# Projection stage of an attention and FFN kernel: a ring of four x tiles in place of two, loads issued four batches ahead

## What is computed

```python
def attn(x):                      # on layernorm(x)
    q, k, v = proj(Wq, bq), proj(Wk, bk), proj(Wv, bv)          # B, H, S, 8
    idx = clip(pos[None, :] - pos[:, None], -20, 20) + 20
    attn1 = einsum('bhqd,bhkd->bhqk', q, k)
    attn2 = einsum('bhqd,qkd->bhqk', q, rel_k[idx])
    attn = softmax((attn1 + attn2) / sqrt(8))
    w1 = einsum('bhqk,bhkd->bhqd', attn, v)
    w2 = einsum('bhqk,qkd->bhqd', attn, rel_v[idx])
    return merge(w1 + w2) @ Wo.T + bo
x = x + attn(layernorm(x))
x = x + ffn(layernorm(x))         # silu(x Wg) * (x Wu), then Wd; weights int / 127
```

## Time and profile before

| | us |
|---|---|
| median of 3 runs | 1351.07 (1350.78 to 1351.37) |
| the profiled execution, its own time | 1343.95 |
| its span, first to last instruction | 1342.2 |
| projection stage, about | 0 to 140 |
| attention, about | 140 to 1180 |
| output, about | 1180 to 1342 |
| busy over the span: PE, DVE, ACT, POOL | 1238.7, 915.1, 755.4, 569.9 |

### The profile page before, as it was taken

How to read it: one execution, slowest core, us unless ns; L and a number is a source line. 1 busy time by engine, 2 the same in 40 slices (tenths; PEclk the granted TensorE clock), 3 DMA queues, 4 the chain that set the end, 5 groups by cost and what they waited for, 6 DMA issues and landing times. The chain is left out here.

```text
span 1342.2 us, 71473 instructions
## 1 busy us (share of the span) xinstructions
PE 1238.7 (92%) x32608; PEld 924.2 (69%) x32608; DVE 915.1 (68%) x1780; ACT 755.4 (56%) x1414; POOL 569.9 (42%) x1047
## 2 busy tenths in 40 slices
PE   4878599999999999999999999999999999999998
PEld 3555267777777777777777777777777777766766
DVE  5766876767777777676777767677777676246664
ACT  5867155656656556565665656566565565623332
POOL 5866345343444444343435343434444443212221
PEclk9989589999999999999999999999999999989999
DMA  4655310111011111102021111121111110022221
GB/s 136 197 186 195 90 31 19 49 30 57 28 48 42 34 46 32 53 24 56 20 56 33 50 38 48 38 56 39 45 42 34 48 28 12 11 57 81 80 86 48
DMA packets 101557, 77.24 MB, mean 58 GB/s; under 512 B 13256, under 2 KB 97032, under 8 KB 101256
## 3 DMA queue, kind: packets, MB, share of 16 engines
q1 hardware_dynamic: 101256, 72.67, 18.4%
HBM read 44.86 MB, written 26.21 MB: 53 GB/s over the span
## 5 line engine op out<-in xcount | busy, mean ns | idle before, releaser
L1117 DVE TENSOR_REDUCE b_mx<-b_a 128x1 f32<-128x512 f32 x1024 | 658.4, 685 | 221.7 <-PE b_a L831 217.5
L1062 ACT ACTIVATE b_p<-b_s 128x512 f32<-128x512 f32 x1024 | 569.9, 596 | 393.8 <-PE b_s L873 308.1
L923 PE MATMUL b_pv<-b_p,vg 128*16 128x128 f32 x8192 | 292.9, 275 | 1.1 <-issue 1.0
L791 POOL TENSOR_TENSOR qd<-q,one 48x512 bf16<-48x512 bf16 x256 | 266.2, 1040 | 27.7 <-POOLq L287 2.8
L873 PE MATMUL b_s<-qd,z 112*128 112x32 bf16 (+1 forms) x6016 | 250.5, 189 | 3.7 <-issue 3.3
L768 POOL TENSOR_TENSOR b_np<-b_db,one 128x16 bf16<-128x16 bf16 x192 | 39.1, 264 | 466.9 <-DVE b_mx L1117 463.9
L831 PE MATMUL b_a<-k,q 48*128 48x512 bf16 x1024 | 203.6, 393 | 31.5 <-DVE b_mx L1117 11.5
L873 PEld LDWEIGHTS b_s<-qd,z 112*128 112x128 bf16 (+1 forms) x6016 | 205.3, 98 | 15.1 <-issue 5.2
L923 PEld LDWEIGHTS b_pv<-b_p,vg 128*16 128x16 f32 x8192 | 200.5, 96 | 20.6 <-issue 2.9
L857 PE MATMUL b_s<-q,k 54*128 54x64 bf16 (+3 forms) x4608 | 188.2, 201 | 6.9 <-ACT b_p L1062 4.5
L857 PEld LDWEIGHTS b_s<-q,k 54*128 54x128 bf16 (+1 forms) x4608 | 126.7, 95 | 92.7 <-PE b_s L857 29.4
(11 more groups left out here) (142 smaller groups left out, 1270.8 us busy)
## 6 DMA issues: line engine op xcount, KB each, us to landing
x<-in_x SPq DMA_DIRECT2D x32, 256.0 KB, 3.3
scratch_qop<-a_parts SPq DMA_DIRECT2D x16, 384.0 KB, 2.5
scratch_kop<-a_parts SPq DMA_DIRECT2D x16, 384.0 KB, 3.2
k<-scratch_kop SPq DMA_DIRECT2D x32, 192.0 KB
q<-scratch_qop SPq DMA_DIRECT2D x32, 192.0 KB
scratch_v<-a_vr SPq DMA_DIRECT2D x16, 256.0 KB, 3.2
k<-scratch_kop SPq DMA_DIRECT2D x32, 128.0 KB
q<-scratch_qop SPq DMA_DIRECT2D x32, 128.0 KB
```

Source lines behind the costliest of these rows:

```text
L791: nc.gpsimd.tensor_tensor(dst, src, one, ALU.mult).then_inc(s["qd_ready"], 1)
L923: nc.tensor.matmul(PV[32 * a:32 * a + V16, g * P:(g + 1) * P], v[:, 0 if t <= i else 1, t, h, :], PR[at.c % 2][:, t, h, :], start=(t == 0 ...
L1062: nc.scalar.activation(out, src, ACT.Exp, scale=SCALE).then_inc(s["p_ready"], 1)
L1117: nc.vector.tensor_reduce(MX[v.c % 2][:, h:h + 1], PA[(n + hp) % NBANK][:, :], AX_X, ALU.max, negate=True).then_inc(s["a_used"], 1)
```

## The change

The projection takes x tiles from a ring of four: the two tiles x and the two tiles xa. Batch b uses tile b mod 4, each tile with a semaphore of its own. SP issues the loads of batches 2 and 3 at the start of the stage, before it waits for anything and before the constants; the load amid the constants goes away. In step n it waits for "xn" of batch n and loads batch n+4. The waits of DVE count the loads of the new semaphores. Nothing else is changed: same instructions, same sizes, same number of loads.

```diff
--- before.py
+++ after.py
@@ -25,6 +25,7 @@
 FC = F // P
 EPS = 1e-5
 NOUT = 2 + 2
+XRING = 4
 
 
 
@@ -244,7 +245,7 @@
 
 
 
-    X, x_in = k["x"], k["x_in"]
+    X, x_in = k["x"] + k["xa"], k["x_in"] + [m.sem(f"a_x_in{p}") for p in range(2, XRING)]
     xn = m.sb("a_xn", [P, T, E])
     xnT = m.sb("a_xnT", [P, S])
     QF = [m.sb(f"a_qf{p}", [P, S]) for p in range(2)]
@@ -288,21 +289,21 @@
         @block.sync
         def _(sp):
             def load_x(at):
-                sp.dma_start(X[at.c % 2][:, :, :],
-                             d["x"][bass.ds(at.count(), 1)].rearrange("o (t p) e -> p (o t) e", p=P)).then_inc(x_in[at.c % 2], 16)
-
+                r = at.count() % XRING
+                sp.dma_start(X[r][:, :, :],
+                             d["x"][bass.ds(at.count(), 1)].rearrange("o (t p) e -> p (o t) e", p=P)).then_inc(x_in[r], 16)
+
+            for b in range(2, XRING):
+                load_x(at0(b))
             sp.wait_ge(s["blank"], 1)
             for n, (dst, src) in enumerate(late):
                 sp.dma_start(dst, src).then_inc(s["late"], 16)
-                if n == 9:
-                    sp.wait_ge(s["xn"], 1)
-                    load_x(at0(2))
 
             def step(at):
                 p = at.c % 2
-                if at.plus(3).exists():
-                    sp.wait_ge(s["xn"], at.count(1, 2))
-                    load_x(at.plus(3))
+                if at.plus(XRING).exists():
+                    sp.wait_ge(s["xn"], at.count(1, 1))
+                    load_x(at.plus(XRING))
                 v, guard = (d[n][bass.ds(at.count(), 1)].rearrange("o p t -> p (o t)") for n in ("v", "guard"))
                 dsts = [d[n][bass.ds(at.count(), 1)].rearrange("o s p t -> p (o s) t") for n in ("qop", "kop")]
                 for n, ready in ((0, "qsplit"), (1, "ksplit")):
@@ -430,7 +431,7 @@
                 if at.since(1):
                     act.wait_ge(s["xT"], at.count())
                 for t in range(T):
-                    ins = nc.scalar.activation(xn[:, t, :], X[at.c % 2][:, t, :], ACT.Identity,
+                    ins = nc.scalar.activation(xn[:, t, :], X[at.count() % XRING][:, t, :], ACT.Identity,
                                                bias=tmp["shift"][:, t:t + 1], scale=tmp["rstd"][:, t:t + 1])
                 ins.then_inc(s["xn"], 1)
 
@@ -541,16 +542,16 @@
                         nc.vector.memset(k["vg"][p][:, 0:VW].rearrange("p (n c) -> p n c", c=V16)[:, :, HD:HD + 1], 1.0)
 
             def statistics(at):
-                p = at.c % 2
+                r = at.count() % XRING
 
                 def link(ins):
                     ins.then_inc(s["stats"], 1)
                     dve.wait_ge(s["stats"], at.count(1, 1))
 
-                dve.wait_ge(x_in[p], at.even(1) * 16 + 16)
+                dve.wait_ge(x_in[r], 16 * (at.count() // XRING + 1))
                 if at.since(1):
                     dve.wait_ge(s["shift"], at.count())
-                layernorm_statistics(nc, X[p], tmp, link, s["var"])
+                layernorm_statistics(nc, X[r], tmp, link, s["var"])
 
             for tile in (z, rkj, slot):
                 ins = nc.vector.memset(tile[:, :], 0.0)
```

## The result

| | before | after |
|---|---|---|
| median of four runs each, us | 1350.92 | 1331.36 (1329.51 to 1333.83) |
| the profiled execution, its own time | 1343.95 | 1329.82 |
| its span | 1342.2 | 1328.1 |
| first attention operation | 140.46 | 125.18 |

The ratio of the medians is 0.9873, 95% interval 0.9847 to 0.9899: 19.6 us faster by the medians, 13.6 to 20.7 by the interval. Forecast were 1335.1 in a range of 1328 to 1341, a gain of 16.0.

The account below looks back on a forecast made before the run. A closed loop through SP (x load, statistics, maxima, guard store, next load) was taken to bound the projection. Gain -17.0 plus store loss 1.0 made -16.0 us, from median 1351.07 to 1335.1, range 1328 to 1341.

Parts of the forecast that it names:

- The loop through SP and its price: Projection: load, statistics, maxima, guard store, load form a closed loop; loading four ahead cuts it, all ten waits go, gain 17.0 us.
- The new period: Projection loop: ACT and PE set the pace next, 6.43 us a batch, 70.7 for eleven, PE's clock at its upper level.
- POOL and the stores: Projection: POOL lags 0.76 us a step with memsets, so ACT waits for stores; 1.0 us lost, bounds 0.3 to 3.3.
- paid once: ACT's q parts in the projection: worst store lateness 0.9 us costs only once, since ACT's delay lets POOL catch up.
- The prologue: Start of projection: loading batches 2 and 3 before the constants removes DVE's 4.58 us wait; gain 0, bounds 0 to 0.5.
- Conversions and bytes: Projection: ACT's three weight conversions, 0.51 us each, cost nothing; 234 GB/s, share 0.72, leaves DMA engines not full.
- The sum: Whole kernel: -17.0 + 1.0 = -16.0 us, subtracted from the median 1351.07, gives 1335.1.
- The return of the clock: Early attention, 141 to 179 us: PE's clock recovery need not slide exactly with the earlier start; +-2 us, taken at 0.
- Hidden anyway: Rival, projection: DVE's idle for x turns into the same idle for another release, time stays 1351; chance 0.04.
- The HBM side slows with load: Rival, projection: every landing grows by 2 us, so the gain is 14.0, time 1337; chance 0.08.
- Stores take over: Rival, projection: heavier DMA traffic and POOL's lag make ACT wait in many steps, gain 10 to 12, about 1340; chance 0.15.
- Slower: Rival, projection: a two-batch loop through the stores loses to today's pace from landings of 10.2 us; example 1357; chance 0.03.

Follow-up runs that it names:

- experiment 2: Kernel before with the ring of four tiles and batch 2 loaded first, other loads still issued three batches ahead; 1343.11 us, ratio 0.9981 to before.
- after_again: The changed kernel run once more without an edit, beside before; 1330.20 us, ratio 0.9870 to before.
- e7: Changed kernel with POOL's six memsets moved to the stage start, steps 13 and 14 and attention's start, none in the setup; 1329.78 us, ratio 0.9867.
- e4: Changed kernel with one more 256 KB load of x each step into a tile nobody reads; 1333.51 us, ratio 0.9890 to before.
- e5: Changed kernel with four more memsets of 1.8 us on POOL, in steps 7 to 10; 1339.26 us.
- e2: Changed kernel with POOL's six memsets moved from steps 1 to 6 into the setup, stage start and steps 13 and 14; 1330.78 us, ratio 0.9886.

## Why the prediction held, step by step

- *The loop through SP and its price.* Right. The ten waits of the earlier trace rows went, the periods of the earlier trace rows became 6.42, and experiment 2 brought waits and long periods back with the distance alone. The distance itself came out shorter than said: 6.35 to 7.55 us for the loads of steps 3 to 9, 8.7 to 9.8 before and behind, instead of 7.4 throughout. SP's stores, and with them the load behind, wait for POOL's q parts.
- *The new period.* 6.43 forecast, 6.42 measured in seven of the eleven periods; the clock stayed at its upper level, as said, in two of the three profiles of the changed kernel. In after_again it was 0.53 from 70 to 73 us, after PE had waited 1.76 us for ACT.
- *POOL and the stores.* The mechanism and the place were right: POOL's first q residuals of batches 4 to 7 were forecast for 51.0, 58.2, 64.6 and 70.9, and are here:

```profile
50.58 1.16 POOL L483 TENSOR_TENSOR a_qr<-a_qf,a_parts 128x512 f32<-128x512 f32 x1
...
58.01 1.16 POOL L483 TENSOR_TENSOR a_qr<-a_qf,a_parts 128x512 f32<-128x512 f32 x1
...
64.38 1.16 POOL L483 TENSOR_TENSOR a_qr<-a_qf,a_parts 128x512 f32<-128x512 f32 x1
...
70.87 1.16 POOL L483 TENSOR_TENSOR a_qr<-a_qf,a_parts 128x512 f32<-128x512 f32 x1
```

The q part of batch 7 was to wait 0.9 us for the stores of batch 5; it waited 1.07. The size of the whole term was off: 1.0 us forecast, 2.05 measured, inside 0.3 to 3.3. I had taken v's landing of 3.2 as the last one. With SP held up by POOL, though, the guard store is issued at once behind v instead of later by itself, and then it lands late:

```profile
62.83 0.53 SPq L313 DMA_DIRECT2D scratch_v<-a_vr  x1
63.41 0.72 SPq L315 DMA_DIRECT2D scratch_guard<-a_gd  x1
```

The trace has the landing of each. In the changed kernel the eight guard stores issued within 0.9 us of v took 2.8 to 3.7 us; of the seven issued 1.7 us or more behind v, six took 1.5 or 1.6 and one 2.9. Those of batches 4 to 7 were issued at 55.65, 63.41, 69.55 and 75.93 and took 2.8, 2.8, 3.5 and 3.7, which gives 58.45, 66.2, 73.05 and 79.6. ACT's q parts two batches later start at 58.51, 66.29, 73.09 and 79.70, each within 0.1 us. The q part of an even period starts 2.60 us behind the copy (58.50 in e7, after 55.90); these four start 2.73, 3.95, 2.96 and 2.77 behind it. The differences, 0.1, 1.35, 0.4 and 0.2, add up to the loss (for the third, an idle of 0.26 us, the profile names PE as the releaser, but PE had delivered the q product more than 1 us before). So the step that was mis-sized is "paid once": the lateness was paid in four steps, by the guard store and not by v. The allowance of 0.1 for stretched operations was small too: POOL's last operation for batch 5's q parts, at 60.36, took 1.50 us where the others take 1.16.
- *The prologue.* Forecast 0 to 0.5, measured 0.3 in the first profile (23.66 against 23.94), but the three profiles of the changed kernel lie at 23.66 to 24.44 and those of before at 23.94 and 24.19, so nothing can be told from it. DVE's wait of 4.58 us is gone.
- *Conversions and bytes.* The conversions are free, as said; e7 shows it. At 227 GB/s no load of x was late; 256 KB more a step (e4) made none late either, but cost 1.7 to 2.1 us through the waits for the guard store.
- *The sum.* With the loss as measured, -17.0 + 2.05 = -15.0 would have been the projection's term; 15.3 was measured at the start of attention, 14.4 to 15.6 over the pairings. The medians gave 19.6, then 17.8 and 14.3. That the 7.1 us between the profiled execution and the median might sit in the projection was a guess of the prediction for the low end of its range; no profile of before's pace shows it there, and attention, which the change does not touch, accounts for about half. The 3.7 us between the forecast and the first measured median are within this scatter. The median alone is therefore a weak test of the mechanism; the periods are the strong one.
- *The return of the clock.* Priced at up to 2 us and taken at 0: 0.2 us in the first profile, but 2.2 in after_again.
- *Rivals.* "Hidden anyway" fell with the result. "The HBM side slows with load" is not what happened: the median landings of x and v stayed at 3.3 and 3.2 us, and only the guard store's grew. "Stores take over" is true for four steps only, and heavily in one, and would need a longer lag or more traffic: e4 and e5 show how it starts. "Slower" is far away; with 254 GB/s the guard's longest landing was 4.7 us, against the 10.2 from which the old pace is reached.

## What to carry over

Read the price of a wait from the period of the engine that sets the pace, not from the idle time of the engine that waits: 26.5 us of DVE idle were worth 17.0. A load that is issued too late for its consumer, in a loop through the issuing queue, repays one step of distance. One step was enough here because the distance, at least 6.35 us, exceeded the landing, 5.1 us for that load. Check this with the distances of the new schedule: they are not the old ones plus a period. Then ask which engine's total work is nearest to the new period; here POOL, at 7.19 against 6.43 in four steps with a long memset, cost 2 us of the gain, and moving its memsets is worth something only where neither POOL nor DVE beside it is needed.

## What was not expected of the hardware

- A stage of a thousand microseconds bound by PE, with the same instructions and a granted clock of 1.00, took 990.2 to 997.8 us in fourteen profiles, and the runs of before in one session spanned 11 us. Four runs that agreed within 1.1 us had not shown this.
- Blocking between POOL and DVE goes both ways and can move a whole stage: 2.25 us for a DVE operation of 0.22 beside a memset of POOL, and, in before, 1.20 us for a POOL operation of 0.20, at 84.91 beside a DVE operation from 84.84 to 86.06.
- The time to landing of a small store (64 KB) was 2.8 to 3.7 us when it was issued within 0.9 us of the last of three large ones, and mostly 1.5 or 1.6 when 1.7 us or more behind. The spacing is not all of it: in e2 two of them, 1.4 us behind, took 3.2 and 3.4.
- The same place of the same kernel can lose the clock or keep it. After a wait of PE for ACT of 1.76 us in after_again and 1.71 in e5 the granted clock was 0.53 and 0.57 from 70 to 73 us; in the first profile of the changed kernel the wait was 2.01 and the clock stayed at 1.00.
